# Two cross attentions of a Perceiver stack: statistics in a batch's last units, stores ahead of the shift rows, and a shorter weight preparation

## The chip, the core and the metric

The kernel runs on one core of a Trainium2 chip, in one launch. The metric is the device time of that launch in microseconds; the profile is one execution taken by the hardware profiler. Engines are called PE (matrix products), DVE (vector), ACT (activations), POOL (GpSimd) and SP (here only an issuer of DMAs).

## What is computed

Sixteen batches of 64 latents of width 128 pass through six stages: cross attention on a context, a selective scan, a block of experts, a second cross attention with a mask, a state space block, and a feed-forward with four-bit rounding. The change is in the two cross attentions. Each computes, per batch, with 16 heads of 64:

```
n  = layernorm(latents)            # twice, see below
c  = layernorm(context)            # 1601 rows of 128; the first attention makes it, the second reads it back
q  = n Wq ;  k, v = [c ; n] Wkv
out = latents + softmax(q k^T / 8 [+ mask]) v Wo
```

## The kernel before

**Folding.** Keys are never made. The kernel forms Wq Wk^T and Wv Wo per head once (`qk_hi`, `qk_lo`, `vo_c`, `vo_l`), so that a query of a head is a 128-wide vector that meets the normalised context rows directly. Layernorm's weight and bias go into fold matrices `F1` (context) and `F2` (latents), made on DVE (L454). Where accuracy needs it, a value is kept as two float16 halves, high and low, and a product is three matmuls.

**Preparation** (`cross_attention`, L337 to L483). PE computes 19 items, each into one of four pairs of PSUM banks: `KF_C, VF_C, KF_L, VF_L` (fold times Wkv, two 512-column products each), the transposed latents `LAT` and `LATX`, the turned Wq, the four turned `kf`/`vf` (`K_C, K_L, V_C, V_L`, eight transposes each), four items `QK` and four `VO`. ACT and DVE share the copies out of PSUM (`by_act`, `by_dve`). At the end PE runs filler matmuls that only keep its clock up (`keep_clock`, L98). In the first attention DVE also takes, between those copies, the statistics of batch 0 (L236 and the chain after it: five aggregate operations, one addition, nine steps of a reciprocal root) and the thirteen `bn_stats` of batch 1. POOL then normalises batch 0 (L264, thirteen tiles) and splits it in halves (L221, L223). SP stores the halves to memory (`store_x`, L205), waits for the landing, and reads them back transposed (`load_xT_front`, `load_xT_rest`, L193) and plain (`load_x`, L188). A block ends when all engines are done with it.

**Attention loop** (`attention_loop`). Context rows come in 13 tiles of 128, each handled as two units of 8 heads; with the latents' own two units a batch has 28 units. In unit u PE makes the scores three units ahead (L786 to L788), ACT takes the exponential twice (`p_hi` L929, in place L930), DVE subtracts to get `p_lo` (L1134), and PE adds the products (L805 to L807). Four score buffers go round. Beside this the next batch is prepared by a hand-made list of items, one or no item a unit, in `items()`: four query items (`q`, once for two batches), sixteen maxima items (`max`, L852 on PE, L1076 or L1073 on DVE), `turn` (a transpose of the maxima, L863), and three output items of the pair before (`out`, L812 and L813, then L1113 and L1119 on DVE). DVE consumes an item one unit after PE made it. The maxima, taken in the order 0, 2, .., 14, 1, 3, .., 15, give a shift per row: DVE adds the constant rows (L1081, after item 13), subtracts the turned maxima (L1092, L1093, L1095), and SP writes the result into row 127 of the queries (`rows`, L729 out, L731 in). The scores of the next batch's first three units, made in its predecessor's last two, need that row.

**The other streams of the first attention.** While batch b is computed, DVE takes the statistics of batch b+2 in its first units (`stats_parts`, parts 0 to 3 in units 0 to 3, the chain up to unit 8), POOL normalises and splits it, and SP, in this order, writes the shift rows, loads the raw rows of b+3 (L179), stores b+2 and waits for its landing, then issues front transposes, rest transposes and the plain load, each when the buffer is free. `before` functions do the same ahead of the first batch. Batches go in pairs: pair 0 is written out, pairs 1 to 5 are a hardware loop (so four branches back), pairs 6 and 7 are written out. The even batch of a pair has the outputs, the odd one the queries. The second attention reads the stored context and has no statistics; its mask makes ACT and the DVE maxima (L1073) a little longer.

The list of items, the part of it that the change touches:

```
out, u = {}, 1 + LEAD[par]
for item in todo:
    out.setdefault(u, []).append(item)
    ...
        u += 1 + {paused: PAUSE[par][0], ("max", 2 * NC_ - 1): PAUSE[par][1]}.get(item, 0)
```

Of the kernel before, what the change touches and what calls it, by code (L numbers as in the profile page):

```python
# [17 lines left out]
P = 128  # L18
# [46 lines left out]
STATS_PARTS = 4 + 2 + RSQRT_STEPS  # L65
# [54 lines left out]
def cross_attention(nc, glob, name, ctx_dram, mask_dram, w_dram):  # L120
# [12 lines left out]
    with ExitStack() as st:  # L133
# [28 lines left out]
        prep_ready, prep_act, prep_dve = sem("prep_ready"), sem("prep_act"), sem("prep_dve")  # L162
# [64 lines left out]
        def context_stats(v, wait, n, par, i, part):  # L227


            if part == 0:  # L230
                x_step[0] = Steps(v, norm_steps, n * NORM_STEPS)
                v.wait_ge(raw_in[par], (i + 1) * 48)
            steps = x_step[0]
            if part < 4:
                for j in range(4 * part, min(4 * part + 4, KT)):
                    steps.mark(v.bn_stats(xstats[:, j, :], raw[par][:, j, :]))  # L236
            elif part == 4:
# [12 lines left out]
            else:  # L250
                steps.wait()
                if part == 5:
                    steps.mark(v.tensor_scalar(xrv[:, :], xvar[:, :], LN_EPS, None, ALU.add))
                else:
                    steps.mark(rsqrt_step(v, part - 6, xr[:, :], xrv[:, :], xrt[:, :]))
            assert part < STATS_PARTS - 1 or steps.n == NORM_STEPS

        def context_normal(pool, wait, n, par):
# [4 lines left out]
            for j in range(KT):  # L263
                ins = pool.tensor_scalar(xt[:, j, 0:D - 1], raw[par][:, j, 0:D - 1], xmean[:, j:j + 1], xr[:, j:j + 1],  # L264
                                         ALU.subtract, ALU.mult)
# [6 lines left out]
        with ExitStack() as pre:  # L272
# [6 lines left out]
            kf_c, kf_l, vf_c, vf_l = (tmp(n, [P, INNER]) for n in ("kf_c", "kf_l", "vf_c", "vf_l"))  # L279
# [12 lines left out]
            by_act = {KF_C: kf_c, KF_L: kf_l, WQ_T: WqT, K_L: kT_l, V_L: vT_l, VO + 1: (vo_c, 8), VO + 3: (vo_l, 8)}  # L292
            by_dve = {VF_C: vf_c, VF_L: vf_l, K_C: kT_c, V_C: vT_c, VO: (vo_c, 0), VO + 2: (vo_l, 0)}
# [6 lines left out]
            def dve_count(n):  # L300
                return sum(k <= n for k in by_dve)

            def read(eng, n):
# [3 lines left out]
                elif n in by_dve:  # L307
                    eng.wait_ge(prep_dve, dve_count(n))
# [17 lines left out]
            def copy_of(n, made):  # L326
                if isinstance(made, tuple):
                    return heads_of(*made), by_heads(n)
                return (made[:, :] if n < LAT else made[:, :, :].rearrange("p g d -> p (g d)")), slot_of(n)


            STATS_WITH = {n: [(b, part) for part in parts] for n, b, parts in (
                (VF_C, 0, range(0, 4)), (VF_L, 0, range(4, 8)), (K_C, 0, range(8, STATS_PARTS)), (VO + 2, 1, range(0, 4)))}
            if masked:
# [2071 lines left out]
```

## Time and profile before

| what | us |
|---|---|
| median of 3 runs | 2179.07 (2177.42 to 2181.53) |
| the profiled execution's own time | 2175.95 |
| its span, first to last instruction | 2174.3 |
| first attention: preparation, stage before the first pair | 7.4 to 53.6, to 88.1 |
| second attention: preparation, stage before the first pair | 1154.9 to 1186.4, to 1216.5 |

A line of the timeline gives start, duration, engine, line, operation, output and inputs, and in brackets the idle time before it with what ended it. Records of one kind in a row are merged (x13). L12 is line 12 of the kernel. SPq rows are DMA issues of SP.

### The profile page before, as it was taken

How to read it: one execution, taken by the hardware profiler on the slowest of the kernel's cores; microseconds unless marked ns; L12 is line 12 of the kernel's file. 1: busy time of each engine (PE TensorE's matmuls, PEld its weight loads, DVE VectorE, ACT ScalarE, POOL GpSimd, SP SyncE). 2: the span in 40 equal slices, each digit the busy share in tenths (PEclk: the TensorE clock that was granted, in tenths of full speed). 3: DMA queues.
4: the chain of work that ended last, by engine and by line, in shares of the span. 5: the costliest groups of instructions: out<-in, count | busy, mean ns of one | idle time of the engine just before them, and what ended most of it. 6: DMA issues, size and time to landing. Idle time of an engine off the chain costs nothing. (4 is left out here: it accounts for less than half of the span.)

```text
span 2174.3 us, 37348 instructions
## 1 busy us (share of the span) xinstructions
PE 2012.8 (93%) x11706; PEld 1090.7 (50%) x11706; DVE 1700.0 (78%) x4108; ACT 1284.3 (59%) x2308; POOL 600.7 (28%) x648
## 2 busy tenths in 40 slices
PE   5899999999999999889798999999999999999886
PEld 4444545353535455433567445454545454544584
DVE  5789797979788887589666877778787979785657
ACT  2376666666666666644323486868687777777211
POOL 3435353534343432059201102121111111110000
PEclk8899999999999999989999899999999999999897
DMA  3222222222222211033104012121111111110100
GB/s 111 81 64 64 65 64 63 64 63 63 63 64 63 91 37 48 9 95 126 48 1 110 5 37 52 31 61 36 35 36 36 36 36 37 36 33 1 27 2 10
DMA packets 148169, 108.91 MB, mean 50 GB/s; under 512 B 120748, under 2 KB 136088, under 8 KB 148024
## 3 DMA queue, kind: packets, MB, share of 16 engines
q1 hardware_dynamic: 148024, 107.26, 17.2%
q8 instruction: 57, 0.93, 0.2%
q14 instruction: 88, 0.72, 0.1%
HBM read 65.15 MB, written 14.29 MB: 37 GB/s over the span
## 5 line engine op out<-in xcount | busy, mean ns | idle before, releaser
L1134 DVE TENSOR_TENSOR x_p_lo<-x_psum,x_p_hi 128x512 f16<-128x512 f32 (+2 forms) x896 | 605.5, 684 | 153.8 <-ACT x_psum L930 141.1
L929 ACT ACTIVATE x_p_hi<-x_psum 128x512 f16<-128x512 f32 (+2 forms) x480 | 287.4, 599 | 303.3 <-PE x_psum L788 301.5
L929 ACT ACTIVATE x_p_hi<-x_psum,x_bcol 128x512 f16<-128x512 f32 (+1 forms) x416 | 288.8, 694 | 139.6 <-PE x_psum L788 137.4
L805 PE MATMUL x_psum<-x_p_hi,x_x_both 128*128 128x512 f16 (+1 forms) x832 | 316.7, 381 | 33.1 <-DVE x_p_lo L1134 32.5
L786 PE MATMUL x_psum<-x_q,x_xT_both 128*128 128x512 f16 x832 | 316.9, 381 | 0.9 <-DMA x_q<-x_shift_rows 0.7
L807 PE MATMUL x_psum<-x_p_hi,x_x_both 128*128 128x512 f16 (+1 forms) x832 | 315.8, 380 | 0.0
L787 PE MATMUL x_psum<-x_q,x_xT_both 128*128 128x512 f16 x832 | 315.8, 380 | 0.0
L806 PE MATMUL x_psum<-x_p_lo,x_x_both 128*128 128x512 f16 (+1 forms) x832 | 315.8, 380 | 0.0
L788 PE MATMUL x_psum<-x_q,x_xT_both 128*128 128x512 f16 x832 | 315.8, 380 | 0.0
L1073 DVE CUSTOM_DVE_ANT_0 x_junk<-x_psum,x_brow 128x512 bf16<-128x512 f32 (+2 forms) x512 | 279.7, 585 | 9.9 <-PE x_psum L852 9.2
L930 ACT ACTIVATE x_psum<-x_psum 128x512 f32<-128x512 f32 (+2 forms) x480 | 286.0, 596 | 0.6
L852 PE MATMUL x_psum<-x_xT_both,x_q 128*128 128x512 f16 (+2 forms) x1024 | 268.9, 340 | 15.0 <-DVE x_mx L1076 3.9
L1076 DVE TENSOR_REDUCE x_mx<-x_psum 128x1 f32<-128x512 f32 (+2 forms) x512 | 276.5, 585 | 6.9 <-PE x_psum L852 6.4
L930 ACT ACTIVATE x_psum<-x_psum,x_bcol 128x512 f32<-128x512 f32 (+1 forms) x416 | 276.2, 664 | 0.2
L264 POOL TENSOR_SCALAR x_xt<-x_raw,x_xmean,x_xr 128x127 f32<-128x127 f32 x208 | 166.5, 816 | 298.1 <-DVE x_xr L85 298.1
L852 PEld LDWEIGHTS x_psum<-x_xT_both,x_q 128*128 128x128 f16 x1024 | 99.0, 97 | 186.7 <-DVE x_mx L1076 48.6
L979 POOL TENSOR_SCALAR x_brow<-x_mrow 128x1536 bf16<-128x1536 uint8 x16 | 36.3, 2266 | 531.6 <-DVE x_shift_rows L1095 479.2
L805 PEld LDWEIGHTS x_psum<-x_p_hi,x_x_both 128*128 128x128 f16 (+1 forms) x832 | 81.0, 97 | 171.7 <-DVE x_p_lo L1134 85.3
L709 POOL TENSOR_TENSOR x_prod<-x_prod 128x1024 f32<-128x1024 f32 (+3 forms) x56 | 67.0, 1197 | 237.1 <-DVE x_prod L1119 233.8
L788 PEld LDWEIGHTS x_psum<-x_q,x_xT_both 128*128 128x128 f16 x832 | 81.4, 98 | 98.6 <-issue 0.3
L807 PEld LDWEIGHTS x_psum<-x_p_hi,x_x_both 128*128 128x128 f16 (+1 forms) x832 | 81.4, 98 | 98.4 <-issue 0.3
L806 PEld LDWEIGHTS x_psum<-x_p_lo,x_x_both 128*128 128x128 f16 (+1 forms) x832 | 81.5, 98 | 79.5 <-issue 0.3
(450 smaller groups left out, 3256.9 us busy)
## 6 DMA issues: line engine op xcount, KB each, us to landing
x_x_both<-context_rows SPq DMA_DIRECT2D x32, 832.0 KB, 5.4
context_rows<-x_x SPq DMA_DIRECT2D x16, 832.0 KB, 5.7
x_raw<-in_ctx SPq DMA_DIRECT2D x16, 768.0 KB
ssm_c_row<-ssm_bc_rows SPq DMA_DIRECT2D x16, 512.0 KB, 4.1
ssm_b_wide<-ssm_bc_rows SPq DMA_DIRECT2D x7, 512.0 KB, 3.5
x_mrow<-in_mask_BxS_bk SPq DMA_DIRECT2D x16, 200.1 KB
x_Wkv<-in_L_xattn_Wkv SPq DMA_DIRECT2D x4, 512.0 KB, 4.9
x_xT_both<-context_rows SPq DMA_TRANSPOSE x96, 3.7
```

Of the source, the lines that this page charges most:

```text
L786: pe.matmul(out, k_hi, q_hi[s][par][:, chunks, :], start=True, stop=False)
L787: pe.matmul(out, k_hi, q_lo[s][par][:, chunks, :], start=False, stop=False)
L788: pe.matmul(out, k_lo, q_hi[s][par][:, chunks, :], start=False, stop=True).then_inc(s_ready, 1)
L805: pe.matmul(out, v_hi, p_hi[r][rows, :], start=start, stop=False)
L806: pe.matmul(out, v_hi, p_lo[r][rows, :], start=False, stop=False)
L807: pe.matmul(out, v_lo, p_hi[r][rows, :], start=False, stop=stop).then_inc(pv_done, 1)
L852: ins = pe.matmul(aux[:, 512 * bank:512 * bank + w], lhs, xT_hi[at.npar][:, k:k + w], start=True, stop=True)
L929: act.activation(p_hi[r][rows, :], score[r][rows, :], ACT.Exp, scale=SCORE_UNIT, **bias).then_inc(p_hi_ready, 1)
L930: act.activation(score[r][rows, :], score[r][rows, :], ACT.Exp, scale=SCORE_UNIT, **bias).then_inc(p32_ready, 1)
L1073: ins = v.tensor_tensor_reduce(junk[:, 512 * bank:512 * bank + w], src, brow[:, w0:w0 + w], 1.0, -3.4e38, ALU.add, ALU.max, m)
L1076: ins = v.tensor_reduce(m, src, AX.X, ALU.max)
L1134: v.tensor_tensor(p_lo[r][rows, :], score[r][rows, :], p_hi[r][rows, :], ALU.subtract).then_inc(p_lo_ready, 1)
```

## The change

1. *Statistics.* The thirteen `bn_stats` are split into five parts of 3, 3, 3, 2 and 2 tiles. In the loop they are taken for batch b+3 in units 23 to 27 of batch b; the chain of batch b+2 then stands in units 2 to 7, two steps a unit, ahead of the unit's item. In the very first batch the parts of batch 2 are in units 0 to 4 and the chain follows.
2. *SP's order.* `rows` is split: the constant rows go out as before, then raw load, store with its wait and front transposes, and only then the shift rows are written. The first batch's store, transposes and load move from the preparation block to the `before` stage, and there the second batch's raw load, store, transposes and load also stand ahead of the shift rows.
3. *Preparation.* `K_C, K_L, V_C, V_L` are computed already turned, as eight 128-column products each; `KF`, `VF` and their transposes go. ACT makes all plain copies. DVE takes all statistics of batch 0 in one go, normalises seven of its thirteen tiles, and POOL the other six. The closing filler is 4 instead of 12.
4. *Smaller things.* L1081 with its wait for the constant rows comes after maxima item 1 instead of 13; the three output items are two units apart; ACT does one tiny exponential at the end of `before`.

```diff
+STATS_OF = ((0, 3), (3, 6), (6, 9), (9, 11), (11, KT))
+AGGR = len(STATS_OF)
+ROOTS = AGGR + 2
+STATS_PARTS = ROOTS + RSQRT_STEPS
...
-            KF_C, VF_C, KF_L, VF_L, LAT, LATX, WQ_T, K_C, K_L, V_C, V_L, QK = range(12)
+            K_C, K_L, V_C, V_L, WQ_T, LAT, LATX, QK = range(8)
...
-                        item(n, [(0, f[:, :], Wkv[:, o + k * 512:o + (k + 1) * 512]) for k in range(2)])
+                        item(n, [(0, Wkv[:, o + g * P:o + (g + 1) * P], f[:, :]) for g in range(8)])
...
-                    keep_clock(pe, slot_of(N_PREP), ident, 12)
+                    keep_clock(pe, slot_of(N_PREP), ident, 4)
...
-                        context_normal(pool, wait_for, 0, 0)
+                        pool.wait_ge(norm_steps, NORM_STEPS)
+                        for j in range(FRONT, KT):
+                            if j == KT - 1:
+                                pool.wait_ge(front_normal, 1)
+                            ins = normal_tile(pool, j, 0)
+                        ins.then_inc(xt_ready, 1)
                         halves(pool, 0)
...
+                    if not masked:
+                        for part in range(STATS_PARTS):
+                            context_stats(v, wait_for, 0, 0, 0, part)
+                        v.wait_ge(norm_steps, NORM_STEPS)
+                        for j in range(FRONT):
+                            ins = normal_tile(v, j, 0)
+                        ins.then_inc(front_normal, 1)
...
-                u += 1 + {paused: PAUSE[par][0], ("max", 2 * NC_ - 1): PAUSE[par][1]}.get(item, 0)
+                u += 1 + {paused: PAUSE[par][0], ("max", 2 * NC_ - 1): PAUSE[par][1], ("out", 0): 1, ("out", 1): 1}.get(item, 0)
...
             def before(at):
                 if masked:
                     load_mask(0, 0)
                     load_mask(1, 1)
-                rows(at)
+                else:
+                    store_x(sp, 0)
+                    load_xT_front(sp, 0, 0)
+                    load_xT_rest(sp, 0, 0)
+                    load_x(sp, 0, 0)
+                rows_out(at)
                 if not masked:
                     sp.wait_ge(xt_ready, 1)
                     load_raw(sp, 2, 0, 1)
                     store_x(sp, 1)
                     load_xT_front(sp, 1, 1)
                     load_xT_rest(sp, 1, 1)
                     load_x(sp, 1, 1)
+                rows_in(at)
...
                 if at.has_next:
-                    rows(at)
+                    rows_out(at)
                 if at.has_next3 and not masked:
                     sp.wait_ge(xt_ready, at.b + 2)
                     load_raw(sp, at.b + 3, at.npar, at.ni + 1)
...
                     load_xT_front(sp, at.b + 2, at.par)
+                if at.has_next:
+                    rows_in(at)
+                if at.has_next2:
                     wait_alone(sp, s_ready, at.half + 2 * KT)
...
+                act.activation(warm[:, :], ident[:, 0:1], ACT.Exp)
...
+            def stats_parts(u, at):
+                rest = [[AGGR]] + [[k, k + 1] for k in range(AGGR + 1, STATS_PARTS, 2)]
+                early = ([[k] for k in range(AGGR)] if at.first and at.par == 0 else [[], []]) + rest
+                late = {LAST - AGGR + 1 + k: [k] for k in range(AGGR)}
+                return early[u] if u < len(early) else (), late.get(u, ())
...
-                    if a == 2 * NC_ - 3:
+                    if a == 1:
```

## Rows read from the trace of the kernel before

**Rows 1.** The page, its first line.

```profile
span 2174.3 us, 37348 instructions
```

**Rows 2.** Windows: stretch and length in us, busy us of each engine, clock, DMA.

```profile
7.40:53.60 46.20, 28.64 (x244) 23.43 (x245) 30.31 (x97) 14.20 (x14) 18.54 (x18) 0.87 0.36 114
...
394.87:500.58 105.71, 100.36 (x579) 49.84 (x578) 88.90 (x209) 66.99 (x133) 43.55 (x47) 1.00 0.21 65
1154.90:1186.40 31.50, 31.04 (x272) 26.29 (x272) 23.10 (x56) 12.70 (x13) 3.16 (x2) 0.95 0.67 177
...
1507.93:1608.55 100.62, 98.83 (x579) 50.41 (x578) 80.37 (x217) 74.75 (x133) 19.11 (x27) 1.00 0.15 39
```

**Rows 3.** Timeline of the first attention's preparation, all engines.

```profile
18.07 2.60 DVE L236 BATCH_NORM_STATS2 x_xstats<-x_raw 128x6 f32<-128x128 f32 x13
...
28.81 0.17 DVE L84 SCALAR_TENSOR_TENSOR x_xrt<-x_xrt,x_xrv 128x13 f32<-128x13 f32 x1
29.01 0.17 DVE L85 SCALAR_TENSOR_TENSOR x_xr<-x_xrt,x_xr 128x13 f32<-128x13 f32 x1
...
29.39 10.43 POOL L264 TENSOR_SCALAR x_xt<-x_raw,x_xmean,x_xr 128x127 f32<-128x127 f32 x13 [21.84 <-DVE x_xr L85]
30.26 4.82 DVE L481 TENSOR_TENSOR x_qk_lo<-x_psum,x_qk_hi 128x1024 f16<-128x1024 f32 x4
...
44.90 0.37 SPq L205 DMA_DIRECT2D context_rows<-x_x  x1
45.93 2.12 POOL L441 TENSOR_TENSOR x_lat_lo<-x_latx,x_lat_hi 128x1024 f16<-128x1024 f32 x1
48.37 4.18 SPq L193 DMA_TRANSPOSE x_xT_both<-context_rows  x3
...
53.62 0.26 PE L832 MATMUL x_psum<-x_lnT_hi,x_qk_hi 128*128 128x128 f16 x1 [14.41 <-PEq L337]
```

**Rows 4.** Timeline of the stage before the first pair, DVE and PE.

```profile
65.51 15.10 DVE L1076 TENSOR_REDUCE x_mx<-x_psum 128x1 f32<-128x512 f32 x30
...
85.03 1.05 DVE L1095 TENSOR_TENSOR x_shift_rows<-x_shift,x_shift_rows 8x256 f16<-8x256 f32 x1
...
88.10 0.39 PE L786 MATMUL x_psum<-x_q,x_xT_both 128*128 128x512 f16 x1 [0.75 <-DMA x_q<-x_shift_rows]
```

**Rows 5.** Timeline around L1081 in an even and an odd batch.

```profile
431.45 3.34 POOL L223 TENSOR_TENSOR x_x<-x_xt,x_x 128x1664 f16<-128x1664 f32 x1 [0.15 <-POOL x_x L221]
...
433.26 1.80 DVE L1081 TENSOR_TENSOR x_shift<-x_const_rows 8x256 f32<-8x256 f16 x1
...
488.16 3.34 POOL L223 TENSOR_TENSOR x_x<-x_xt,x_x 128x1664 f16<-128x1664 f32 x1 [0.15 <-POOL x_x L221]
...
496.71 0.40 DVE L1081 TENSOR_TENSOR x_shift<-x_const_rows 8x256 f32<-8x256 f16 x1
```

**Rows 6.** Timeline of PE in the first batch.

```profile
97.77 0.54 PE L852 MATMUL x_psum<-x_xT_both,x_q 128*128 128x512 f16 x2 [1.87 <-issue]
```

**Rows 7.** Windows: the start of the second pair, columns as in rows 2.

```profile
195.50:199.00 3.50, 3.50 (x10) 1.24 (x10) 2.48 (x9) 1.08 (x2) 0.00 (x0) 0.51 0.95 230
```

**Rows 8.** Waits of PE from 100 to 900 us, and timelines at two branches back.

```profile
PE x_psum L805 <- DVE x_p_lo L1134: 22.9, 32, 1.2
...
398.60 0.58 ACT L930 ACTIVATE x_psum<-x_psum 128x512 f32<-128x512 f32 x1
...
401.61 0.69 DVE L1134 TENSOR_TENSOR x_p_lo<-x_psum,x_p_hi 128x512 f16<-128x512 f32 x1 [4.24 <-ACT x_psum L930]
...
1513.46 0.69 DVE L1134 TENSOR_TENSOR x_p_lo<-x_psum,x_p_hi 128x512 f16<-128x512 f32 x1 [3.03 <-issue]
```

**Rows 9.** Timeline of DVE at an output item.

```profile
442.90 1.02 DVE L1119 TENSOR_TENSOR x_prod<-x_psum,x_rec 128x384 f32<-128x384 f32 x2
```

**Rows 10.** Timeline of ACT at the second attention's first exponential.

```profile
1217.43 1.28 ACT L929 ACT_TABLE_LOAD   x1 [24.55 <-PE x_psum L788]
```

**Rows 11.** Waits of SP: us in total, times, longest.

```profile
SPq L731 <- DVE x_shift_rows L1095: 923.9, 32, 31.0
```

More of the change, by code:

```diff
@@ L328, in copy_of @@
                     return heads_of(*made), by_heads(n)
[L329 to L334, printed above, removed]
-                STATS_WITH = {}
+                return made[:, :, :].rearrange("p g d -> p (g d)"), slot_of(n)
             with nc.Block() as block:
@@ L368, in item @@
                         for k, (fn, a, b) in enumerate(parts):
-                            if len(parts) == 8 and not fn:
+                            if by_pairs:
                                 k = k // 2 + 4 * (k % 2)
@@ L427, in _ @@
                             act.activation(heads_of(qk_hi[k // 2], 8 * (k % 2)), by_heads(n), ACT.Copy).then_inc(qk_hi_ready, 1)
+                            if k == 1:
+                                act.wait_ge(lnT_ready, 1)
+                                act.activation(lnT_hi[:, :], lnT[:, :], ACT.Copy).then_inc(lnT_hi_ready, 1)
                 @block.gpsimd
@@ L483, in _ @@
-                        for b, part in STATS_WITH.get(n, ()):
-                            context_stats(v, wait_for, b, b, 0, part)
+                    if not masked:
+                        for part in range(AGGR):
+                            context_stats(v, wait_for, 1, 1, 0, part)
         attention_loop(nc, glob, name, st, sb, sem, psum, locals(), mask_dram, context_stats, context_normal)
@@ L721, in row_of, with rows_out @@
                 return q[P - 1:P, :, :]
-            def rows(at):
+            def rows_out(at):
                 if at.npar == 0:
@@ L1122, in before @@
             def before(at):
+                if not masked:
+                    for part in range(AGGR, STATS_PARTS):
+                        context_stats(v, wait_alone, 1, 1, 0, part)
                 for item in at.index:
                     consume(at, item)
-                    if item == ("q", Q_ITEMS - 1) and not masked:
-                        for part in range(4, STATS_PARTS):
-                            context_stats(v, wait_alone, 1, 1, 0, part)
             def body(at):
@@ L1136, in body @@
                         latents_sums(at.half, 1 - at.par)
-                    soon, later = stats_parts(u) if at.has_next2 and not masked else ((), ())
-                    for part in soon:
+                    two, three = stats_parts(u, at) if not masked else ((), ())
+                    for part in two if at.has_next2 else ():
                         context_stats(v, wait_alone, at.b + 2, at.par, at.i + 1, part)
@@ L1144, in body @@
                             consume(at, item)
-                    for part in later:
-                        context_stats(v, wait_alone, at.b + 2, at.par, at.i + 1, part)
+                    for part in three if at.has_next3 else ():
+                        context_stats(v, wait_alone, at.b + 3, at.npar, at.ni + 1, part)
             every(v, before, body)
```

83 lines of the change are left out of this document (32 added, 51 removed).

## The prediction, made before the changed kernel was built

> **What bounds it now.** The page comes first, for the span of 2174.3 us [rows 1]. The stretches then show that PE is the busy engine, and where it is not [rows 2]. A pair of contexts in the first attention's loop takes 105.7 us, the same pair in the second's 100.6 us with nearly the same PE work (100.4 and 98.8 us busy), so PE sets both and waits a few us in each. The first preparation is different: 46.2 us, PE busy for 28.6. Its timeline [rows 3] shows the block ending on SP: DVE frees the root at 29.01, POOL normalises until 39.8, SP can store at 44.90, waits for the landing, and spends 4.18 us issuing transposes and then a load; PE's next block starts at 53.6, after 14.4 us of nothing. After that the first score waits for the sixteen maxima on DVE and the shift rows, to 88.1 [rows 4].
>
> **First preparation.** DVE now takes the thirteen statistics straight after the latents, from about 18.0, where the raw rows are already there: 2.6 us, 0.9 for the five aggregates (estimate), ten chained steps 0.21 apart (28.81, 29.01), so the root stands at 23.4 where it stood at 29.2. POOL takes six tiles of 0.80 (10.43 / 13), to 28.4, the two halves 1.57 and 3.34, to 33.4, and its two latent halves 3.2, to 36.7. On PE eight 128-column products replace two 512-column ones at equal columns, 1.8 us for each of four items; four groups of eight transposes and four copies go, so PE is not the end. DVE is: seven tiles in about 2, two latent steps in 2.6, four qk_lo and lnT_lo at 1.2 each (4.82 / 4), then 2.6 of the second batch's statistics: with short waits 37.2 (an estimate). One thing can hold it. lnT_lo reads two SBUF tiles, and would start near 30, beside POOL's 3.34 us subtraction. L1095, of the same kind, took 1.05 beside a POOL subtraction [rows 4] and L1081 1.80 where 0.40 is usual [rows 5]. I take the collision, plus 2.7: block end at 39.9, between 37 and 43. Term: 53.6 less 39.9 is **-13.7**.
>
> **Stage before the first pair.** SP stores at once, 3.5 to landing, 4.2 of transposes, and a load of about 0.6; the transposes land before the maxima start. The statistics chain (2.8) now lies beside the queries instead of between them and the maxima, and PE's pause is short, so its clock should stay up. Maxima start at +8.5 (it was +11.9), take 16.0 (15.10 for 30 of 32), L1081 about 1.0 beside POOL, and 2.9 to the shift rows: +28.4. What the new order puts ahead of the shift write in SP's queue: POOL normalises batch 1 from +3.2, ends its halves at +18.8, store and landing +22.5, three transposes and a load +27.4. So SP is free just in time; a landing of 5.7 us would cost 1.3. The write follows an 832 KB load: 2 to 4 us, taken as 3. First score at +31.4 against +34.5: **-3.1** (from -5 to +1).
>
> **First two pairs.** Batch 1's transposes were issued at 94.15, and PE stood until 97.77 for them [rows 6]; in the new order they are issued 20 us earlier. With the raw rows the same, and the start of the second pair had a like wait, where the clock fell to half for 3.5 us [rows 7]. I take 2.0 and 3.5 off. First-body statistics stay where they were. New costs as in the next part, about 1.5: **-4.0** (from -8 to 0).
>
> **Pairs in the loop and the one behind it, five.** Here I find the change costing, not paying. A unit is one step of 512 columns for scores and outputs, 1.3 us of PE, 1.62 to 1.68 with a maximum.
> (a) Gain at the start of an even body: 2.6 us of statistics left DVE's fullest units. PE waits for low parts 22.9 us in the first loop [rows 8]; by matmul starts, which lie 0.22 us apart when nothing waits, 2.9 us of a pair go in units 1 to 8. The chain, two steps a unit, keeps about 0.75. -2.2.
> (b) Cost at the end of an odd body. Late statistics add three tiles (0.59) to units 23 to 25, two (0.39) to 26 and 27. PE has only 0.65 us of work in unit 25, so the last low parts come 1.1 us later, and DVE's last instruction 2.8 us later. The row at 401.61 shows what follows: DVE comes back 4.24 us after its last instruction although ACT had released it at 399.2, and in the second attention 3.03 us with no releaser [rows 8]. This is the branch back, and it shifts with the last instruction. With the raw load and store gone from that moment it may shrink toward the masked value. Next low part 1.6 to 2.8 us later for PE: +2.2 for four branches, about nothing at the fifth, which falls through.
> The Trainium skill (Advanced Engine Details and Errata, Control Flow Timing) gives a compare-and-branch about 108 ns; by it (b) would keep 1.1 and the pair would gain 1.1 more. The row of this case says otherwise, and I use the row.
> (c) L1081 moves six odd units of 1.62 us forward, 9.7 us. In even bodies it ran into POOL's L223 (433.26, 1.80 us) [rows 5]; now it falls among the 0.80 us tiles: -1.2, with up to 0.8 given back. In odd bodies it ran free at 496.71; it comes to 487.0, while POOL, freed 2.9 us earlier, has L223 from 485.3 to 488.6. There it now waits: +1.1 net of the 0.33 us it leaves near the turn.
> (d) Outputs two units apart: each projection (0.28 and 0.94 us) [rows 9] no longer holds the next output, but holds the next low part: 0 net without statistics. With 0.59 us of statistics behind it the low parts of units 24 and 26 come 1.0 and 0.7 us late, against 0.9 now: +1.3.
> Sum of a loop pair: -2.2 + 2.2 - 1.2 + 1.1 + 1.3 = +1.2; four such, and about +0.7 for the pair behind: **+5.5** (from -6 to +12).
>
> The Trainium skill (SBUF — State Buffer, Who interferes with whom) says that a VectorE instruction with two SBUF inputs blocks for the whole of a GpSimd instruction that reads SBUF. For L223 the rows agree. No row shows it for the normalising tiles; by the rule (c) loses 0.4 us more per even body, some 3 us over the kernel.
>
> **Second attention.** Preparation, 31.5 us: four groups of eight transposes (about 0.9 us each, an estimate) leave PE's chain and the closing filler shrinks from 12 matmuls to 4: the block ends near 1182 instead of 1186.4, **-4.4** (from -2 to -6). The exponential's table, 1.28 us ahead of the first exponential [rows 10], goes under the maxima: **-1.3**. Its loop has no statistics; L1081 leaves the units before the turn, where by matmul starts 0.3 to 0.5 us are lost, for units with little slack: 15 bodies at 0.2, **-3.0** (from -7 to +1). The spread outputs give nothing by (d). The SP order there only puts front transposes ahead of the shift write: each waits at most 1.4 us and is not needed for 10.
>
> **Sum.** -13.7 - 3.1 - 4.0 + 5.5 - 4.4 - 1.3 - 3.0 = **-24.0**. The profiled execution took 2175.95 us and would take 2152; the median of the runs is 3.1 higher, so I predict **2155**. A measurement can tell about 0.2%, 4.4 us, from no change.
>
> **Rivals.**
> *The loops gain* (0.15). If the back branch shortens to 3 us and L1081 misses L223, each of five pairs saves 1 to 3 us: 2155 less 12 is 2143. For: the odd-body collision needs a match within 1.5 us. Against: both ends hang on the same unit 7.
> *The pause lowers the clock* (0.12). After 3.2 us of waits within 6 us the granted clock was 0.51 for 3.5 us [rows 7]; in the loop pair of [rows 2] the same sort of waits, spread wider, left it at 1.00. A single wait of 2.5 to 3.5 us at four boundaries could tip it, at 1.7 us each, and more in the two stages before the loops, where the filler is cut: 2155 + 9 = 2164.
> *The preparation's gain is hidden* (0.06). If DVE or POOL hold the block to 48, or the shift write waits behind landing and load, 12 us of the 17 go: 2167.
> *Slower* (0.05). SP's queue: the shift write now stands behind halves, store, landing (5.9 us) and front transposes. It decides if POOL finishes more than 10 us later than I place it, since the score needs the rows only at unit 26. Fourteen bodies at 3 us would give 2197; from 1.7 us a body the kernel is slower. Against: the shift write waits for DVE for 923.9 us in all today [rows 11], so SP has room.
> *The order does nothing* (part of 0.62): the transposes were waited for only in the first pairs, which the forecast already says.
>
> **Range and chances.** The forecast with its bounds (2147 to 2163) has 0.62. 2140 to 2168 takes in two rivals and most of the third. Faster 0.91, same 0.04, slower 0.05.
>
> **What would show it.** Right: PE's next block after the preparation at 37 to 43, first score at 68 to 75, a DVE pause of over 3 us still at each back branch, loop pairs of 105.5 to 108 us; L1081 at 0.4 to 1.2 us in even bodies and near 1.8 in odd; no table load before the first masked exponential. Wrong: loop pairs under 104.5, a clock under 1.00 inside the loop, SP's shift write later than 3 us behind L1095, or DVE idle in the preparation.

## The result: 2179.94 to 2146.61 us, and the profile after

The kernel before took 2179.94 us (median of 4 runs, 2177.42 to 2181.53), the changed one 2146.61 (4 runs, 2143.31 to 2151.68): a ratio of 0.9847, 95% interval 0.9825 to 0.9869. The profiled execution of the changed kernel took 2143.31 us. The head of its page, to be read against [rows 1]:

```profile
span 2141.6 us, 37339 instructions
PE 1999.5 (93%) x11706; PEld 1085.6 (51%) x11706; DVE 1694.3 (79%) x4103; ACT 1289.5 (60%) x2314; POOL 599.4 (28%) x641
```

Line numbers are higher than in before: the shift sum L1081 is L1094 here, POOL's subtraction L223 is L226, DVE's low parts L1134 are L1147. Four stretches of the changed kernel, as [rows 2] has them of before: the first preparation up to PE's next block, a pair in the first loop (first score to first score), the second preparation, a pair in the second loop.

```profile
7.40:37.60 30.20, 25.30 (x244) 24.25 (x244) 25.81 (x98) 15.88 (x16) 14.17 (x11) 1.00 0.38 127
374.21:479.35 105.14, 99.85 (x580) 50.07 (x579) 90.17 (x209) 67.12 (x132) 43.97 (x49) 1.00 0.22 65
1129.50:1156.80 27.30, 25.99 (x272) 25.32 (x272) 16.13 (x50) 14.44 (x15) 3.17 (x2) 0.94 0.80 204
1477.75:1577.87 100.12, 98.97 (x580) 50.13 (x579) 80.07 (x217) 74.75 (x132) 19.18 (x28) 1.00 0.15 39
```

The preparation went from 46.2 to 30.2 us; the first loop's pair lost only half a microsecond and still holds 5.3 us of waits. One table says where the 32.6 us of the span went. A body is one batch's turn in the loop, numbered from 0, so bodies 4 and 5 make pair 2. The table takes the start of the first score matmul of a body in both traces and subtracts:

| up to | before | after | gained here | forecast |
|---|---|---|---|---|
| PE's next block after the preparation | 53.6 | 37.7 | 15.9 | 13.7 |
| first score | 88.10 | 69.97 | 2.2 | 3.1 |
| body 4 (two pairs) | 291.29 | 269.01 | 4.15 | 4.0 |
| last score of the first attention | 902.66 | 876.88 | 3.5 | **-5.5** |
| first score of the second | 1216.53 | 1186.07 | 4.7 | 4.4 |
| its last score | 1997.52 | 1963.07 | 4.0 | 4.3 |
| end | 2174.26 | 2141.62 | -1.8 | 0 |

ACT's load of the exponential's table, 1.3 us of the forecast, is counted behind the second attention's first score, where it stood before. Nearly all of the difference to the forecast lies between body 4 and the first attention's last score, 9.0 us. The last row is no part of the change: no code there differs. The two stretches below, of before and then of after, start at like places in the last outputs:

```profile
2002.50:2009.30 6.80, 6.78 (x61) 6.80 (x62) 2.38 (x8) 0.00 (x0) 0.00 (x0) 1.00 0.01 2
```
```profile
1968.00:1974.80 6.80, 6.73 (x45) 6.76 (x46) 1.27 (x4) 0.00 (x0) 0.00 (x0) 0.75 0.01 2
```

The granted clock was 1.00 (2.4 GHz) in one and 0.75 on average in the other, half of it at 1.2 GHz, and 16 fewer matmuls ran. From the last score to the end the kernels of this study take 176.4 to 181.8 us with the same code; from the last score of the first attention to the first of the second, the changed kernel took 309.2 and others with the same code there 310.5 to 314.6. So a difference of whole times under 5 us is read here by marks inside a trace, not by its end.

**The preparation.** DVE and then POOL in the changed kernel:

```profile
22.66 0.17 DVE L88 SCALAR_TENSOR_TENSOR x_xr<-x_xrt,x_xr 128x13 f32<-128x13 f32 x1
22.88 1.90 DVE L265 TENSOR_SCALAR x_xt<-x_raw,x_xmean,x_xr 128x127 f32<-128x127 f32 x7
29.46 1.51 DVE L481 TENSOR_TENSOR x_lnT_lo<-x_lnT,x_lnT_hi 128x1024 f16<-128x1024 f32 x1
33.16 2.60 DVE L242 BATCH_NORM_STATS2 x_xstats<-x_raw 128x6 f32<-128x128 f32 x13
37.89 0.18 DVE L249 TENSOR_TENSOR x_xd<-x_xstats 128x13 f32<-128x13 f32 x1 [2.14 <-PEq L335]
```
```profile
29.98 4.21 POOL L226 TENSOR_TENSOR x_x<-x_xt,x_x 128x1664 f16<-128x1664 f32 x1
35.25 2.12 POOL L439 TENSOR_TENSOR x_lat_lo<-x_latx,x_lat_hi 128x1024 f16<-128x1024 f32 x1
```

The root stands at 22.8 (23.4 forecast). lnT_lo and POOL's subtraction did meet, but DVE was first by half a microsecond: it took 1.51 us (1.23 in the kernel before) and POOL's took 4.21 instead of 3.34. The block ends on POOL, at 37.4.

**The transfers**, SP's queue:

```profile
37.67 0.37 SPq L208 DMA_DIRECT2D context_rows<-x_x  x1
41.15 4.30 SPq L196 DMA_TRANSPOSE x_xT_both<-context_rows  x3
60.05 4.16 SPq L196 DMA_TRANSPOSE x_xT_both<-context_rows  x3
67.21 0.70 SPq L734 DMA_DIRECT2D x_q<-x_shift_rows  x1
```

The second batch's transposes are issued at 60.05 where PE once waited for those of 94.15 [rows 6]; that wait is gone. The shift write goes out as soon as DVE is done (67.18), so nothing was lost by moving it behind the rest.

### The profile page after: what moved, and what is told of

Same layout as the page of the kernel before. It is cut to its first block and busy times, and to the rows that moved or that the text cites. A ratio compares the mean times of both kernels' runs of the same rounds, so it can differ in the third digit from the quotient of the medians.

```text
span 2141.6 us, 37339 instructions
## 1 busy us (share of the span) xinstructions
PE 1999.5 (93%) x11706; PEld 1085.6 (51%) x11706; DVE 1694.3 (79%) x4103; ACT 1289.5 (60%) x2314; POOL 599.4 (28%) x641
## 5 line engine op out<-in xcount | busy, mean ns | idle before, releaser
L1147 DVE TENSOR_TENSOR x_p_lo<-x_psum,x_p_hi 128x512 f16<-128x512 f32 (+2 forms) x896 | 603.4, 681 | 124.5 <-ACT x_psum L942 120.5
```

The lines of the kernel that those rows point to most:

```text
L1147: v.tensor_tensor(p_lo[r][rows, :], score[r][rows, :], p_hi[r][rows, :], ALU.subtract).then_inc(p_lo_ready, 1)
```

## The experiments

Twelve kernels. The columns: median of 4 runs; ratio, with its 95% interval, to runs of the kernel before taken beside it (their medians were 2178.1 to 2178.8 us for e1 to e13); and from the trace of each the first score, the time from the first to the last score of the first attention, and a pair in either loop (first score of body 12 less that of body 4, by four).

| kernel | us | ratio | first score | first attention | pair 1 | pair 2 |
|---|---|---|---|---|---|---|
| before | 2179.94 | | 88.10 | 814.56 | 105.56 | 100.62 |
| after | 2146.61 | 0.9847 (0.9825-0.9869) | 69.97 | 806.91 | 105.14 | 100.16 |
| e1 | 2153.32 | 0.9880 (0.9864-0.9897) | 69.72 | 812.44 | 105.51 | 100.59 |
| e2 | 2129.20 | 0.9767 (0.9748-0.9787) | 69.00 | 791.66 | 102.73 | 100.01 |
| e3 | 2151.15 | 0.9866 (0.9849-0.9882) | 69.78 | 810.70 | 105.91 | 100.45 |
| e5 | 2135.52 | 0.9802 (0.9784-0.9820) | 69.43 | 799.55 | 103.45 | 99.80 |
| e6 | 2141.83 | 0.9837 (0.9818-0.9856) | 69.74 | 802.47 | 104.27 | 100.14 |
| e7 | 2125.90 | 0.9759 (0.9732-0.9786) | 70.00 | 787.70 | 102.20 | 100.13 |
| e8 | 2122.45 | 0.9753 (0.9732-0.9775) | 70.42 | 782.37 | 100.92 | 99.86 |
| e9 | 2133.39 | 0.9800 (0.9777-0.9824) | 69.72 | 793.74 | 103.05 | 100.30 |
| e10 | 2136.71 | 0.9811 (0.9792-0.9830) | 69.34 | 795.33 | 102.82 | 100.01 |
| e11 | 2132.06 | 0.9799 (0.9774-0.9824) | 70.10 | 791.87 | 102.78 | 100.03 |
| e12 | 2132.32 | 0.9795 (0.9774-0.9816) | 70.03 | 794.74 | 103.48 | 100.15 |
| e13 | 2132.70 | 0.9792 (0.9772-0.9811) | 74.13 | 791.76 | 102.75 | 100.26 |

**e1_prep_only.** The changed kernel with everything in the bodies put back.

```diff
-                rest = [[AGGR]] + ...            # stats_parts: late tiles
+                if u < 4: return (u,), (4,) if u == 3 else ()
-    ("out", 0): 1, ("out", 1): 1
-                    if a == 1:
+                    if a == 2 * NC_ - 3:
+                    rows_in(at)                   # body: right behind rows_out
```

> The kernel after with everything inside the bodies put back as before: statistics in units 0 to 3, SP's shift rows ahead of the stores, the shift sum at the fourteenth maximum, outputs one unit apart. The new preparation, the new order of the stage before the first pair and the early exponential table stay. Theory (each part pays by itself, and the loop's parts together are worth little): first score at 70.0 us as in the kernel after (18.1 ahead of before), pairs in the first loop at 105.5 as before, the second attention's preparation 5 us shorter and its loop as before; in all 24 to 27 us under the kernel before, near 2154. Rival (the parts in the bodies are what pays, the preparation's gain is lost in the first pairs, where transfers for batches 2 and 3 are late): first two pairs give back over 4 us, and the time is above 2158. Second rival (the body's parts together cost time, as forecast): under 2146.6, the kernel after's time.

2153.32 us, first score 69.72, pairs 105.51. The new preparation and stage are worth their 18.4 us up to the first score, give nothing back, and the loop is the old one. The parts in the bodies together bring the rest: both rivals are wrong.

**e2_stats_early.** Only the statistics put back in units 0 to 3 (stats_parts and STATS_OF as in the kernel before).

> The kernel after with only the statistics put back in units 0 to 3 of the body behind. A pair in the first loop takes 105.2 us in the kernel after. By the forecast the late statistics cost 1.3 net a pair (gain 2.2 at the start of the even body, cost 2.2 at the branch because the pause moves with DVE's last instruction, 1.3 at the outputs): a pair would take 103.9, and the kernel be 6 us faster than the kernel after. Rival, from the trace of after: the pause hangs on the branch record, which now lies 1.6 us ahead of DVE's last instruction, so the late statistics hide part of it; then the start of the even body loses 2.2, the end of the odd body gains 1.0, the outputs gain 1.1: a pair at 105.1 to 105.5, the kernel within 2 us of after. In this kernel the pause after DVE's last instruction at a branch should be back above 4 us under both.

2129.20 us, pairs of 102.73: **the late statistics cost 2.4 us a pair and 15.3 us over the first attention**. Both expectations were too high. A list of PE's gaps (start to start of the matmuls less 0.216 us each) in one loop pair, changed kernel against e2: start of the even body 1.33 and 1.49; at the outputs and the end of the even body 1.71 and 0.63; at the shift sum of the odd body 1.37 and 0.73; end of the odd body 1.27 and 0.16. Nor is DVE's pause above 4 us, as both had it: it stands idle for 2.84 us and is back 3.5 us behind the branch. The start of the even body, which had been put down to the statistics, is as short with the statistics in it. What did relieve it is the next question.

**e3_outputs_close.** The changed kernel without `("out", 0): 1, ("out", 1): 1`.

> The kernel after with outputs one unit apart as before. Forecast: spreading them beside late statistics costs 1.3 us a pair in the first attention and nothing in the second: pairs of 103.9 and 100.2, the kernel 6 to 8 us faster than the kernel after. Rival from PE's gaps in the trace of after (0.42, 0.79 and 0.50 us at the outputs against 0.47 and 0.26 before): 0.5 to 1.0 a pair, 3 to 6 us. Second rival (the spreading is what makes the room for projections): pairs longer by 0.5 or more in both attentions, the kernel 5 us or more slower than after.

A miss for all three: pairs of 100.45 in the second loop, 0.3 longer, and 105.91 in the first, where one body of 56.07 us holds a drop of the clock (0.97 in it); the even bodies without it are 0.6 longer and the odd ones 0.4 shorter, so 0.2. Spreading the outputs pays a little even beside late statistics.

The drop stands right behind a branch back: PE waited 1.48 us for DVE's low part, and from 592 to 594 us the granted clock was 0.50 (1.2 GHz). That body is 2.1 us longer than its like.

```profile
591.21 0.60 PE L817 MATMUL x_psum<-x_p_hi,x_x_both 128*128 128x512 f16 x1 [1.48 <-DVE x_p_lo L1147]
```
```profile
592.00:594.00 2.00, 2.00 (x6) 0.76 (x5) 1.93 (x8) 0.02 (x1) 0.00 (x0) 0.50 0.73 270
```

**e5_unrolled.** The changed kernel with `for i in range(1, PAIRS - 2)` for `with eng.Fori(1, PAIRS - 2) as i`.

> The kernel after with both loops over pairs written out, so that no engine branches back. If the pause of DVE at the branch is what the start of an even body waits for, even bodies in the first attention shrink from 53.4 to 51.7 us (what the sixth, behind the loop, takes) and in the second from 50.8 to 50.4: 4 x 1.7 + 4 x 0.4 = 8.4 us, near 2138. Rival (the gaps at the start of the even body come from its own DVE and ACT work): no change over 1 us. Second rival (the pause is the fetch of instructions, which straight code must make too, with four times as many instructions and in competition with the data): gaps spread over the bodies, no gain or slower.

2135.52 us, even bodies of 51.66 in the first attention and 50.43 in the second, as expected: 11.1 us by the medians, 9.4 by the two stretches from first to last score (7.4 and 2.1). Straight code brought no new gaps. The pause at a branch is PE's loss of 1.7 us in the first attention and 0.4 to 0.5 in the second.

**e6_early_sp_old.** e2 with SP's order in the bodies put back.

```diff
                 if at.has_next:
                     rows_out(at)
+                    rows_in(at)
...
-                if at.has_next:
-                    rows_in(at)
```

> The kernel e2_stats_early with SP's order inside the bodies put back: shift rows ahead of raw load, store and front transposes. Theory (instruction fetch): at each branch back DVE has to fetch 8 KB of instructions, and that fetch waits behind data in the DMA engines. In before and in e1_prep_only, where SP issues the raw load and the store 6 to 7 us ahead of DVE's branch, the fetch starts 2.75 to 2.9 us behind the branch and DVE is back 4.6 us behind it; in e2_stats_early 1.35 and 3.4. So here: 2.8 and 4.6 again, the gaps at the start of an even body back from 1.5 to about 3.0 us, a pair of 102.75 us in the first loop at 104.2 to 104.5, the kernel 6 to 7 us slower than e2_stats_early. Rival (it was the shift sum or the outputs that shortened the pause and the chain behind it): pair within 0.3 of 102.75. Second attention unchanged under both (50.6 and 49.35 a body).

2141.83 us, pairs of 104.27, and 10.8 us more over the first attention, of which 3.1 in body 2. So SP's order is what shortened the start of the even body. But the expectation named one cause, and the even body of pair 6, the first pair behind the loop and with no branch back ahead of it, lost 1.5 us too (53.27 for 51.78). DVE there:

```profile
686.75 0.69 DVE L1146 TENSOR_TENSOR x_p_lo<-x_psum,x_p_hi 128x512 f16<-128x512 f32 x1 [1.85 <-ACT x_psum L941]
688.39 0.87 DVE L242 BATCH_NORM_STATS2 x_xstats<-x_raw 128x6 f32<-128x128 f32 x4 [0.95 <-DMA x_raw<-in_ctx]
```

The raw rows, loaded behind the shift write, land after DVE wants them, and its next low part waits behind. DVE waits for them in this way in bodies 2 and 12 alone (1.33 and 0.95 us), the two that no branch back leads to.

**e12_raw_ahead_store_behind.** e2 with rows_in between load_raw and store_x, to split the two causes.

> The kernel e2_stats_early with the shift rows between raw load and store inside the bodies: raw rows are early, as there, but the store of 832 KB and its transposes come behind the shift rows, at DVE's branch, as in e6_early_sp_old. It splits that kernel's 1.5 us a body. If the fetch of DVE's instructions behind data is the cause: DVE is back 4.4 to 4.8 us behind its branch, even bodies in the loop take 54.2 to 54.9 and the sixth pair's even body, which has no branch in front, 51.8. If late raw rows are the cause: branch pause may be long but even bodies stay at 53.0, and the sixth at 51.8. If both: 53.6 to 54.2. Since front transposes come late too, the next maxima may wait for them, as a third part, seen as a PE wait on DMA.

Even bodies of 53.7 in the loop and 51.79 in pair 6. With the raw rows early pair 6 loses nothing, and behind a branch 0.7 us remain of the 1.2 to 1.9. So there are two causes, each in its own place: late raw rows where no branch back is ahead, and a longer pause of DVE where one is. There the raw load counts too, though DVE never waits for its rows: with raw load and store behind the shift write (e6) DVE is back 4.6 to 5.0 us behind the branch, with the store alone (e12) 4.1 to 4.2, with neither (e2) 3.4 to 3.5. DVE's first low part behind the branch in e1 (which has e6's order of SP), then e2, e12 and the changed kernel:

```profile
484.87 0.69 DVE L1146 TENSOR_TENSOR x_p_lo<-x_psum,x_p_hi 128x512 f16<-128x512 f32 x1 [4.07 <-ACT x_psum L941]
```
```profile
472.19 0.69 DVE L1147 TENSOR_TENSOR x_p_lo<-x_psum,x_p_hi 128x512 f16<-128x512 f32 x1 [2.84 <-ACT x_psum L942]
```
```profile
475.56 0.69 DVE L1147 TENSOR_TENSOR x_p_lo<-x_psum,x_p_hi 128x512 f16<-128x512 f32 x1 [3.55 <-ACT x_psum L942]
```
```profile
481.22 0.49 DVE L242 BATCH_NORM_STATS2 x_xstats<-x_raw 128x6 f32<-128x128 f32 x2
484.16 1.29 DVE L1147 TENSOR_TENSOR x_p_lo<-x_psum,x_p_hi 128x512 f16<-128x512 f32 x2 [2.45 <-ACT x_psum L942]
```

The branch records lie at 480.2, 468.7, 471.4 and 480.1, so DVE is back 4.7, 3.5, 4.2 and 4.1 us behind them. Not all of it is the branch's. Where e2 leaves the loop and nothing branches back, and at the same place of the unrolled e8, DVE stands idle for 1.84 us, waiting for ACT:

```profile
676.66 0.69 DVE L1147 TENSOR_TENSOR x_p_lo<-x_psum,x_p_hi 128x512 f16<-128x512 f32 x1 [1.84 <-ACT x_psum L942]
```
```profile
467.55 0.69 DVE L1147 TENSOR_TENSOR x_p_lo<-x_psum,x_p_hi 128x512 f16<-128x512 f32 x1 [1.84 <-ACT x_psum L942]
```

The first of them starts 2.5 us behind the branch that isn't taken (674.18), so a branch back costs DVE 1.0 us more in e2 and 2.2 more in e1. What it waits for then is in the DMA view. From the branch of e1 to 482.85, and of e2 to 470.0:

```profile
DMA packets 178, 0.82 MB, mean 309 GB/s; under 512 B 15, under 2 KB 48, under 8 KB 178
q1 hardware_dynamic: 178, 0.82, 87.9%
```
```profile
DMA packets 597, 0.15 MB, mean 118 GB/s; under 512 B 597, under 2 KB 597, under 8 KB 597
q1 hardware_dynamic: 597, 0.15, 54.0%
```

Data alone in both. The next packet of the other kind comes at 482.90 and 470.06, one of 8 KB of instructions; the same view up to 472.1 of e2 has it:

```profile
q14 instruction: 1, 0.01, 0.8%
```

DVE resumes some 2 us behind that packet in both, and so it does at 94 of the 96 branches back of all kernels (1.9 to 2.3 us). The packet itself starts 2.7 to 3.1 us behind the branch in e6 and 2.7 to 2.8 in e1, with raw load and store in the DMA engines; 2.2 to 2.3 in e12, with the store; 1.35 to 1.5 in e2, with transposes. That a busy DMA delays it is read from these steps; a kernel with no data at all at the branch wasn't tried.

**e7_early_sum_by_parity.** e2 with the shift sum in odd bodies back at maxima item 13, which is the fifteenth in order (the expectation calls it the fourteenth), and in even ones at item 1, the ninth.

```diff
-                    if a == 1:
+                    if a == (2 * NC_ - 3 if isinstance(at, At) and at.par else 1):
```

> The kernel e2_stats_early with the shift sum at the fourteenth maximum in odd bodies alone, where the early place runs into GpSimd's subtraction (1.95 us for 0.40), and at the ninth in even ones. Theory: the gap of 0.73 us of PE in the odd body goes, pair at 102.0 to 102.2, kernel 3 to 4 us faster than e2_stats_early, near 2126. Rival (PE was held there by the maximum's own chain and not by the sum): no change. In the second attention, which has no such subtraction, odd bodies at 49.4 as before instead of 49.35.

Pairs of 102.20, odd bodies 49.13 for 49.72: 0.6 us each, seven in all, and 0.1 lost in the odd bodies of the second attention. As expected. The medians differ by 3.3. In the changed kernel the shift sum stands beside tiles in even bodies and in POOL's subtraction in odd ones, and ends 0.27 us behind the end of that subtraction:

```profile
399.03 0.40 DVE L1094 TENSOR_TENSOR x_shift<-x_const_rows 8x256 f32<-8x256 f16 x1
461.46 1.95 DVE L1094 TENSOR_TENSOR x_shift<-x_const_rows 8x256 f32<-8x256 f16 x1
```
```profile
459.80 3.34 POOL L226 TENSOR_TENSOR x_x<-x_xt,x_x 128x1664 f16<-128x1664 f32 x1 [0.16 <-POOL x_x L224]
```

In e2 the collision that e7 takes away is a milder one. With early statistics the sum stands in POOL's cast, one instruction earlier, and again ends 0.28 us behind it:

```profile
452.78 1.18 DVE L1094 TENSOR_TENSOR x_shift<-x_const_rows 8x256 f32<-8x256 f16 x1
```
```profile
452.11 1.57 POOL L224 CAST x_x<-x_xt 128x1664 f16<-128x1664 f32 x1 [0.16 <-POOL x_xt L265]
```

**e8_e7_unrolled.** e7 with both loops written out.

> The kernel e7_early_sum_by_parity with both loops over pairs written out, so without any branch back. Theory (the branch's fetch is what is left at the start of an even body, 53.0 us against 51.8 in the sixth pair, which lies behind the loop): 4 x 1.2 in the first attention, 4 x 0.2 in the second, so 5 to 6 us under e7_early_sum_by_parity, near 2120. Rival (straight code has its own fetches, which cost as much here as the branch): within 2 us of it.

The fastest of all, 2122.45 us, 24 us under the changed kernel. Even bodies 51.80 and 50.42, as expected; 6.1 us by the spans, 3.5 by the medians. Its two pairs:

```profile
364.29:465.19 100.90, 99.66 (x579) 49.83 (x579) 87.17 (x209) 66.97 (x132) 43.67 (x48) 1.00 0.23 69
1457.04:1556.90 99.86, 98.67 (x580) 50.07 (x579) 80.25 (x217) 74.71 (x132) 19.17 (x28) 1.00 0.16 40
```

PE now waits 1.2 us in either.

**e9_early_outputs_close.** e2 with outputs one unit apart.

> The kernel e2_stats_early with outputs one unit apart as before. Forecast: nothing, since without late statistics a projection holds either the next output or the next low part. Rival from PE's gaps (0.63 us at the outputs in e2_stats_early, 0.94 in e1_prep_only, and 50.78 against 51.08 us a body in the second attention of after and of e3_outputs_close): 0.3 us more in each even body but the first of either attention, so 4 us slower than e2_stats_early, near 2133.

Pairs of 103.05 and 100.30, each 0.3 longer: the rival, not the forecast.

**e10_stage_rows_first.** e2 with rows_in right behind rows_out in the stage before the first pair.

> The kernel e2_stats_early with SP's order changed back in the stage before the first pair alone: shift rows ahead of the third batch's raw load and of the second batch's store and transposes. Forecast: in this stage the order costs or gains the first score 1 us at most, and the second batch's transposes come some 10 us later, for which PE waits 2.0 us in the first body. Theory after e6_early_sp_old (raw rows that arrive late hold DVE, and with it every low part): the first score within 0.7 us of 69.0, the first body at 45 to 48 us for 42.93 (before: 47.4), the kernel 2 to 5 us slower than e2_stats_early. Rival (the first body's gain comes from the preparation): 43 to 44.

First score 69.34, first body 46.27 for 42.93, and next to nothing behind: 3.3 us, as the theory has it. But the body holds two new gaps of PE, of 1.6 and of 2.1 us (less a gap of 0.5 that goes). The first is the raw rows again, and the second is the transposes' wait of the kernel before [rows 6], which DVE then passes on:

```profile
73.59 0.87 DVE L242 BATCH_NORM_STATS2 x_xstats<-x_raw 128x6 f32<-128x128 f32 x4 [1.47 <-DMA x_raw<-in_ctx]
79.68 1.15 DVE L1089 TENSOR_REDUCE x_mx<-x_psum 128x1 f32<-128x512 f32 x2 [1.68 <-PE x_psum L864]
```
```profile
75.57 4.17 SPq L196 DMA_TRANSPOSE x_xT_both<-context_rows  x3
79.26 0.54 PE L864 MATMUL x_psum<-x_xT_both,x_q 128*128 128x512 f16 x2 [1.96 <-issue]
```

PE's maximum starts 3.7 us behind the transposes' issue; in the kernel before it was 3.6 (94.15 and 97.77).

**e11_no_warm.** e2 without the early exponential.

> The kernel e2_stats_early without the early exponential. Forecast: 1.3 us more in the second attention, where the table is loaded ahead of its first exponential, since all kernels with it have a first body of 41.6 to 41.9 us there and before has 42.9; expected 42.9, kernel 1.3 us slower. Rival: the load only moved under the maxima, where it held something else, and the sum from the end of the queries to the second body is the same within 0.3.

First body of the second attention 42.87 us for 41.59. The table load in e11, and where the changed kernel has it:

```profile
1173.37 1.28 ACT L941 ACT_TABLE_LOAD   x1 [24.82 <-PE x_psum L800]
```
```profile
1163.54 1.28 ACT L947 ACT_TABLE_LOAD   x1
```

It lies under the maxima in the second. The rival asks for the sum, and that doesn't settle it: from the first maximum to the second body e11 takes 66.7 us, and the eleven kernels of this study with the early load and four fillers 64.1 to 66.2. What speaks for a gain of the whole 1.3 is that ACT stands idle for 24.8 us where the load now lies. The medians differ by 2.9 us, which is more than the marks show and within their spread.

**e13_filler_12.** e2 with `keep_clock(pe, slot_of(N_PREP), ident, 12)` for 4.

> The kernel e2_stats_early with twelve filler matmuls for four at the end of both preparations. Forecast: part of the 4.4 us of the second preparation, eight matmuls of some 0.22 us, 1.8 us more between its start and the first maximum (35.7 to 37.9 us in all kernels with four), nothing in the first, which ends on DVE and POOL. Rival: they keep the clock up in the stage behind them and give back as much: the stretch from the preparation's start to the first score within 0.5 us of 59.7 us.

In the second preparation, counted from the end of the stage ahead of it, the first maximum comes 1.9 us later than in e2 (37.1 for 35.2), as expected, and the first score 0.6 (60.4 for 59.8), near the rival's bound. The stage behind the preparation ran at a granted clock of 0.83 for 0.78 in e2; but two kernels with four fillers had 0.82 there, so that the fillers keep it up is not shown. The first preparation was the surprise: the first score came at 74.13, 5.1 us late. DVE and POOL there:

```profile
31.12 3.15 DVE L481 TENSOR_TENSOR x_lnT_lo<-x_lnT,x_lnT_hi 128x1024 f16<-128x1024 f32 x1
```
```profile
29.84 3.35 POOL L226 TENSOR_TENSOR x_x<-x_xt,x_x 128x1664 f16<-128x1664 f32 x1
```

PE's fillers in e13, then in e2:

```profile
38.35 3.86 PE L101 MATMUL x_psum<-ident 128*128 128x128 f32 x24
```
```profile
34.22 1.16 PE L101 MATMUL x_psum<-ident 128*128 128x128 f32 x8
```

PE delivered the latents 1.2 us later than in e2, DVE came to lnT_lo after POOL had begun, and this time DVE waited: 3.15 us. The fillers stand behind all that, so the late latents are not their doing, and why PE was late stays open. DVE's next steps, PE's items behind them and the twelve fillers then ended last, at 42.2, where in e2 POOL ends the block at 37.2. Of the 5 us, 2.7 are the longer filler and the rest is PE coming late to it. Without the collision twelve fillers would end at 38.1 (34.22 + 3.86, an estimate), 0.9 behind POOL. The median is 3.5 us above e2's.

## Why the prediction was right, and its step that was wrong

The forecast was 2155 us for 2146.61 measured, 24.0 us to be gained for 33.3. The time lies 0.4 us under the bounds that the forecast gave its own case (2147 to 2163) and inside its wider range. The form of the gain, most of it in the two preparations and the stage behind, was right. By its terms:

**First preparation, -13.7.** Measured -15.9. The chain of the root, the seven tiles and the order of events are as worked out. The collision at lnT_lo is real, but which engine waits hangs on half a microsecond: in the changed kernel POOL paid 0.87 us and DVE 0.3, in e13 DVE paid 1.9. The 2.2 us are this term's error.

**Stage, -3.1 (-2.2) and first two pairs, -4.0 (-4.15).** The shift sum took 2.11 us beside POOL, the maxima came a microsecond earlier than forecast, and SP was free in time. The first two pairs were right in sum by luck. Their even bodies gained 3.6 and 5.5 us, for 2.0 and 3.5 forecast, and their odd ones lost 2.2 and 2.7, for 1.5 in all. In the first body PE's wait for transposes was as forecast (2.1 us in e10); the 1.6 us for raw rows beside it were missed.

**Five pairs, +5.5.** Measured -3.5 up to the last score: -0.4 for each of the four pairs in the loop (its even body 3.1 us shorter, its odd one 2.7 longer), -1.3 for pair 6 and -0.5 for the last. This is the step that failed, and it failed by its parts:
- (a) *"The chain, two steps a unit, keeps about 0.75. -2.2."* The gaps at the start of an even body were put down to DVE's load of statistics. e2 has that load in the same units and PE's gaps there are 1.49 us, e1 has 3.1. e6 and e12 show the cause: SP's order, which put raw load and store into the DMA engines when DVE branches back, and lengthened its pause. The forecast thought of it ("it may shrink toward the masked value") and gave it nothing in the sum; it is worth 1.5 us a pair.
- (b) *"it shifts with the last instruction."* It doesn't. The pause hangs on the branch record, and in the changed kernel 1.6 us of instructions issued ahead run on behind that. Late statistics cost at the end of the odd body 1.1 us by this, not 2.2. Nor do the 4.24 us of [rows 8] belong to the branch alone: 1.84 of them DVE waits for ACT without any branch (e2, e8).
- (c) right in kind and place: 0.40 us in even bodies, 1.95 in odd ones, exactly where the start of POOL's subtraction was forecast to meet it. The even body's gain was over 1.2 (PE's gaps of 1.25 and 0.45 us there in e1 are gone), the odd body's cost 0.6 in e2 over e7 (the cast) and as much again in the changed kernel over e2 (the subtraction), 1.2 where 1.1 was forecast.
- (d) +1.3 for outputs and late statistics together; 1.1 at this place by the gaps. By e3 the spread has no part in that cost. That it alone gives nothing was wrong: 0.3 us a pair in both attentions (e9).
- The +0.7 for the pair behind the loop doesn't follow: without the branch of (b) the terms give -1.0, and pair 6 measured -1.3.

Late statistics therefore cost 2.4 us a pair where (a), (b) and (d) gave them 1.3; the shift sum, the spread and SP's order bring 2.8 where the forecast had 0.1. The forecast's rival "the loops gain" named a nearer sum (2143) and two mechanisms that don't carry it: the branch shortened from 4.7 to 4.1 us, but L1094 did not miss the subtraction.

The Trainium skill (Advanced Engine Details and Errata, Control Flow Timing) gives 108 ns for a compare-and-branch, and the row was rightly preferred. The rule that would have helped is another one: the Trainium skill (Runtime: NRT & Kernel Launch, Instruction fetch mechanics) says that a taken branch whose target is not at hand forces a DMA fetch before execution goes on. The traces agree: an instruction packet starts 1.3 to 3.1 us behind each branch back, and DVE goes on behind it. e5 and e8 bear out what the section says of full unrolling. That data in the DMA engines delays the fetch comes from the traces alone.

**Second attention, -8.7 in all.** Measured -8.7 (4.7 and 4.0), and that is luck in part. From the preparation's start to the first score before took 62.8 us, the changed kernel 57.7, and the experiments with the same code 57.7 to 60.4, 59.6 in the middle: so 2.5 to 5.1 us, by where the clock fell, for 4.4 forecast. The table load's 1.3 is seen in the first body (42.87 us in e11, 41.59 in e2). The loop's 3.0 was put down to the shift sum, with nothing for the spread. From first to last score e2 takes 775.9 us, e9, without the spread, 777.9, and e1, with the old place of the sum and SP's old order as well, 779.7. So the spread brings about 1.9 us there and the other two together as much; the changed kernel, with e2's code in that stretch, took 777.0, so about 1 us of this is scatter.

**The pause lowers the clock** (0.12) did not happen in the changed kernel: from 64.5 to 894 us the granted clock stays at 1.00, and the drop of [rows 7] is gone too. It did in e3, at one of four branches back and for 2.1 us, so the rival was a real one.

**Signs.** Block end at 37.7, first score at 69.97, L1094's times and the table load were as announced. The pause over 3 us "still at each back branch" was not quite: DVE stands still 2.4 us, since its last instructions cover part. Loop pairs of 105.14 lie just under the 105.5 announced.

## What to carry to other kernels

A gap at the top of a loop body has several possible authors: the work that stands there, an input that lands late, and the branch itself. Before moving the work, look for a DMA releaser on the instruction that follows, for what the DMA engines carry when the branch is taken, and for what the engine would wait for without the branch. Changes that were measured as one gain can hide a part that costs: here the late statistics gave back 15 of some 49 us, and only taking the parts off one at a time showed it. Move transfers that nobody waits for away from the branch, and write a short loop out where the code allows.

## What the runs showed of the hardware

- In the first attention's loop DVE's first instruction behind a branch back starts 3.4 to 5.0 us after the branch record, of which 2.5 pass without a taken branch as well where the statistics are early (e2, e8); ACT's and POOL's sequencers go on after 0.3. An 8 KB instruction packet starts 1.35 to 1.5 us behind DVE's branch when transposes run (e2), 2.2 to 2.3 us when a store of 832 KB does (e12) and 2.7 to 3.1 when the raw load does too (e6). DVE goes on some 2 us behind that packet.
- A port collision has a side: DVE's lnT_lo took 1.51 us when it came first, 3.15 when POOL's subtraction of 3.34 us had begun; POOL's took 4.21 in the first case. The Trainium skill (SBUF — State Buffer, Who interferes with whom) says that issue order decides who blocks, which the forecast left out, and these two traces agree. Beside a normalising tile they don't: in the changed kernel the shift sum took its usual 0.40 us though the tile had begun 0.12 us before it, and the tile 1.06 for 0.80 (398.91 to 399.97). So POOL paid, and the 3 us that the forecast worked out from that page did not come.
